# An adaptive LoRA and feed-forward kernel in split fp32: a sum ahead of a split in the first pair, a low-rank product ahead of the tails' mixing in the second, VectorE's filling increments left out

## The reference

```python
# layer 1: y = x W^T + 2 * sum over the two best experts of gate * (x A_e^T) B_e^T
logits = x @ Wr.T + 5.0 * one_hot(language)        # 8 experts
topw, topi = top_k(logits, 2)
gates = softmax(topw) put at topi
y = x @ W.T + 2.0 * einsum(x @ A, gates, B)        # rank 16
# layer 2: 4 experts, all of them weighted by a softmax
g = softmax(y @ Wr2.T)
z = y @ W2.T + b + 2.0 * einsum(y @ A2, g, Bm)     # rank 8
return x + z
```

## Time and profile before

| what | value |
|---|---|
| median of three runs | 327.86 us |
| the profiled execution, its own time | 328.54 us |
| its span, first to last instruction | 326.8 us |
| TensorE matmuls busy | 319.5 us, 98% |
| TensorE weight loads busy | 314.0 us, 96% |
| VectorE busy | 245.4 us, 75% |
| ScalarE busy | 128.2 us, 39% |
| mean granted clock of TensorE | 0.997 of full speed |
| share of TensorE in the chain that ended last | 94% |

### The profile page before, as it was taken

The page is one execution under the profiler, slowest core; times in us unless marked ns, Lnnn a source line. Parts: engine busy times, 40 slices in busy tenths (PEclk is TensorE's granted clock), DMA queues, the critical chain, the costliest instruction groups (busy, mean ns, idle before and its releaser), DMA issues.

```text
span 326.8 us, 5993 instructions
## 1 busy us (share of the span) xinstructions
PE 319.5 (98%) x2255; PEld 314.0 (96%) x2255; DVE 245.4 (75%) x541; ACT 128.2 (39%) x253; POOL 1.4 (0%) x11
## 2 busy tenths in 40 slices
PE   7999999999999999999999999999999999999994
PEld 6999999999998998899999999999999999999993
DVE  3989999998899778978866856857666685684442
ACT  4872846495148226226413503512431350341120
POOL 1000000000000000000000000000000000000000
PEclk9999999999999999999999999999999999999998
DMA  7999000000000311700420340150061024003004
GB/s 230 421 406 299 6 2 0 2 0 2 0 2 0 130 39 37 252 0 0 143 118 0 76 181 0 52 205 0 0 196 61 0 75 182 0 0 128 0 0 129
DMA packets 10559, 27.56 MB, mean 84 GB/s; under 512 B 3150, under 2 KB 4430, under 8 KB 10544
## 3 DMA queue, kind: packets, MB, share of 16 engines
q1 hardware_dynamic: 10256, 27.18, 24.0%
q10 hardware_dynamic: 288, 0.19, 0.2%
HBM read 18.97 MB, written 8.39 MB: 84 GB/s over the span
## 4 chain that ended last, share of the span: by engine, by line
PE 94%; DVE 2%; DMA 1%; ACT 1%; issue 0%; SPq 0%; DVEq 0%
PE sums L1273 94%; DMA in<-part 1%; PE sums L1512 1%; DVE rows L1048 0%; DVE st_low L771 0%; DVE vt_plain L1214 0%; ACT vt L527 0%; ACT y_exp L719 0%; DVE a_low L771 0%; DVE v L1203 0%; ACT a_high L527 0%; SPq L430 0%; SPq L428 0%; DVE sec L1194 0%; DVE y_half L1200 0%
## 5 line engine op out<-in xcount | busy, mean ns | idle before, releaser
L1273 PE MATMUL sums<-b_high,a_high 128*128 128x256 f32 (+1 forms) x224 | 45.5, 287 | 1.0 <-DVE a_low L771 1.0
L1273 PE MATMUL sums<-b_low,a_high 128*128 128x256 f32 (+1 forms) x224 | 45.4, 286 | 0.0
L1273 PE MATMUL sums<-b_high,a_low 128*128 128x256 f32 (+1 forms) x224 | 45.3, 286 | 0.0
L1273 PEld LDWEIGHTS sums<-b_high,a_high 128*128 128x128 f32 x224 | 34.7, 189 | 1.5 <-DVE a_low L771 1.2
L1273 PEld LDWEIGHTS sums<-b_low,a_high 128*128 128x128 f32 x224 | 34.8, 189 | 0.0
L1273 PEld LDWEIGHTS sums<-b_high,a_low 128*128 128x128 f32 x224 | 34.7, 188 | 0.1
L1048 DVE TENSOR_TENSOR rows<-sums,rows 128x354 f32<-128x354 f32 x48 | 24.4, 521 | 9.7 <-PE sums L1273 9.3
L1273 PE MATMUL sums<-t_high,s_high 128*128 128x354 f32 x96 | 31.6, 330 | 0.0
L1273 PE MATMUL sums<-t_low,s_high 128*128 128x354 f32 x96 | 31.1, 324 | 0.0
L1273 PE MATMUL sums<-t_high,s_low 128*128 128x354 f32 x96 | 31.1, 324 | 0.0
L1048 DVE TENSOR_TENSOR narrow<-sums,narrow 128x244 f32<-128x244 f32 x30 | 12.4, 412 | 24.3 <-PE sums L1273 24.3
(11 more groups left out here) (150 smaller groups left out, 823.0 us busy)
## 6 DMA issues: line engine op xcount, KB each, us to landing
stage<-tokens SPq DMA_DIRECT2D x14, 512.0 KB, 4.0
out<-rows SPq DMA_DIRECT2D x14, 512.0 KB, 4.7
in<-part SPq DMA_DIRECT2D x7, 585.0 KB, 8.4
in<-part SPq DMA_DIRECT2D x4, 777.0 KB, 15.7
in<-part SPq DMA_DIRECT2D x4, 265.0 KB, 18.6
rows<-tokens SPq DMA_DIRECT2D x2, 512.0 KB, 15.8
c_plain<-gate_proj SPq DMA_DIRECT2D x1, 544.0 KB, 17.8
c_plain<-gate_proj SPq DMA_DIRECT2D x4, 136.0 KB, 3.0
```

The costliest lines, as they stand in the source:

```text
L1273: return nc.tensor.matmul(out_, lhs, rhs, start=start, stop=stop, skip_group_check=True)
```

## The change

`STEPS` becomes 10, which is the number of links, and the increments that filled up to 14 go. In the first pair `add_r22` now comes before `split_x(j + 1, 0)` on VectorE; in the second it stays where it was, ahead of `split_tn(T4)`. On TensorE the second pair now has lora for bank B ahead of the tails' mixing, as the first had.

```diff
@@ -1047,7 +1047,7 @@
             def add_sums(dst, n, onto):
                 return nc.vector.tensor_tensor(dst, n, onto, ALU.add)
 
-            STEPS = 14
+            STEPS = 10
             BLOCK = 32
 
             def pair(j, first=False, second=False, last=False):
@@ -1218,13 +1218,13 @@
                     add_r22()
                 dve.wait_ge(v_rounded, j + 1)
                 low_part(vt[ER2:2 * ER2, :, :], vt_plain[:, :, :], vt[0:ER2, :, :]).then_inc(vt_ready, 1)
+                if not steady:
+                    add_r22()
                 if second:
-                    add_r22()
                     split_tn(T4)
                 if not last:
                     split_x(j + 1, 0)
                 if first:
-                    add_r22()
                     next_s(S1)
                     next_s(S2)
                 if second:
@@ -1257,9 +1257,7 @@
                     split_s(j + 1, S3)
                 dve.wait_ge(c_done, j + 1)
                 add_sums(rows[:, 0, wide_at(1)], bank(BANK_C), rows[:, 0, wide_at(1)]).then_inc(c_out, 1)
-                assert step[0] <= STEPS, step
-                for _ in range(STEPS - step[0]):
-                    dve.sem_inc(vec, 1)
+                assert step[0] == STEPS, step
 
             pair(0, first=True)
             pair(1, second=True)
@@ -1547,7 +1545,7 @@
                     pe.wait_ge(t_split, T4 + 1)
                 pe.wait_ge(u3_read, j + 1)
                 of_x(BANK_B, 1, 1, t_high[T4], t_low[T4], False).then_inc(p4_done, 1)
-                if first:
+                if not steady:
                     lora(BANK_B, 1, 0)
                     mixed_tails(j)
                 else:
```

## The result

The changed kernel takes 326.49 us (median of six runs, 326.01 to 326.84) against 327.86 us (six runs, 327.74 to 328.24); the ratio is 0.9953, 95% interval 0.9943 to 0.9964. It is faster by 1.37 us by the medians, and by 1.2 to 1.9 us by the interval of the ratio. I had forecast 326.92 us and a range down to 326.65.

What follows compares the result with a forecast made beforehand. TensorE, busy for 98% of the span, was taken to bound the kernel, so only its standstills could be won. The terms 0.69 + 0.25 + 0 = 0.94 us, off the median 327.86, gave 326.92 us, range 326.65 to 327.45.

Steps and rivals of the forecast that it cites:

- Part 1: First pair: add_r22 ahead of the split of x on VectorE removes TensorE's wait; 0.69 us, bounds 0.45 and 0.7.
- The restart: First pair, TensorE's step behind the wait at product 3: 0.24 instead of 0.16 us, so 0.08 us more gained.
- The bare 0.61 us: Gain in the first pair's stretch, product 4 to product 3, if the weight load were done in the gap.
- Part 2: Second pair: lora ahead of mixed_tails on TensorE makes the wait for vt vanish; 0.25 us, bounds 0 and 0.3.
- What is late next: Logits before the gate: wanted at 139.47, VectorE free at 139.44, so the first pair's gain passes with 0.03 us spare.
- The first rival: Second pair's VectorE list falls behind the earlier TensorE; gain 0.45 to 0.65, time 327.2 to 327.4 us; chance 0.18.
- The second: Second pair: the tails' mixing finds another wait or vt comes later; gain 0.69, time 327.17 us; chance 0.05.
- the fourth: TensorE meets u3_read of the second pair without slack; freed VectorE gives 0.1 to 0.3 more, 326.7 us; chance 0.05.
- Part 3: Four filling increments fewer per pair on VectorE, 32 in a run: costed at nothing, upper bound 0.38 us per pass.
- The third rival: Shorter VectorE program exposes a late fetch now hidden at 127 to 140 us; 2.9 us, time 329.8; chance 0.04.

## Why the prediction was right on both moves and wrong on the increments

**Part 1** was right: 0.69 us forecast, 0.66 measured between the transposes, 0.67 in the run with this part alone. The restart was part of it, as the step of 0.17 us in place of 0.24 shows. The bare 0.61 us that I gave for a weight load done in the gap is less than both measurements.

**Part 2** was right: 0.25 forecast, 0.24 measured, both in the whole change and alone. The copy of the tails started at 153.69 in the changed profile and held nobody up.

**What is late next** was right, to the hundredth of which it spoke: the logits came at 139.49 on the old scale, forecast 139.47, and VectorE had just ended. With 0.03 us to spare, that nothing was held back was partly luck. The first rival, a gate chain that holds the gain back, didn't come: TensorE has no wait behind 7 us. The second and the fourth did not come either. The first narrow matmul of pair 2 stands at 156.55, with the start's 0.55 added 157.10, as forecast. (The chances that I added up for "faster" come to 0.71, not 0.73.)

**Part 3** failed. The term was "I cost them at nothing", with a bound of 0.38 us per pass "and VectorE isn't on the path there". On TensorE's path that is so: 205.22 us with 14 and with 10 steps, 205.24 with 26. On VectorE the bound turned out to be about the whole cost: at the seam of two passes leaving four increments out saved 0.41 us (0.90 to 0.49). The 0.43 us from 132.20 to 132.63 that spoke for no cost are the end of the first pair, not the second's, and hold outside the loop only. What I took for the whole path was TensorE's; the 4.7 us behind it, the last output and the wait for it, I took as a constant that lies around the sum. There 16 instructions fewer in VectorE's text are worth 0.56 us (10 steps alone, ratio 0.9983; and 0.9970 against 0.9953 with both moves).

I had the mechanism in hand and put it at the wrong place with the wrong sign. The third rival says that a shorter text moves a fetch of VectorE's program and that this could make things *slower*, with one in the middle of the run coming into the open. I read the packet from 127 to 140 us, which is one of `q8`, a queue that VectorE's text doesn't move. The packet that mattered is one of `q14`, in the last 5 us, where its removal could only help. A view from 240 to 327 us, taken before the prediction, had listed it, without its place; I didn't ask further. With the half microsecond that the runs give this term, the sum would have been 0.94 + 0.5 and the time 326.4 us.

Of the Trainium skill's passage that I named there (Advanced Engine Details and Errata, ISA Cache: lines of 16 KB or 256 instructions, two of them held) the runs show only that text is fetched in blocks: 48 instructions more in VectorE's text clear the end again and 12 more than the changed kernel's bring the packet back, in line with a border whose place was not located. The packets of this queue carry 8 KB (14 GB/s over 0.6 us), half of the line that the page gives.

Added up: 0.90 us from the moves and 0.5 to 0.6 from the fetch are 1.4 to 1.5 us; the medians say 1.37, the ratio of the first runs 1.5 and that of the repeated ones 1.5. The 0.55 us at the start of the profiled execution are not the change's.

**What stays open.** That the packet carries VectorE's text is inferred from what moves it, not read from its content. That it shares a DMA engine with the late packets is inferred from their times; the engines are not shown one by one. What sets the packet's moment is known in part: it starts at 1.7 us where nothing stands behind the last sum and at 2.1 us with four increments there, but at 2.5 us with four in the changed kernel. There is one profile of each kernel (two of the changed one), so how far packet and end vary between executions of one kernel is not known; whether the larger remainder with 26 steps (0.9 us) differs from 0.6 can't be told from these intervals.

## What to carry to other kernels

Where TensorE is full, the gain of a reordering is the excess of its stretch over the same stretch in an undisturbed pass of the loop, restart included. This gave both moves to 0.03 us. The path doesn't end with the last matmul: ask for the DMA queues of the last few microseconds too, and look for an instruction packet among the packets of the last output. If there is one, a change in the length of an engine's program, even instructions that do nothing, can move it away, and any edit that changes a length should be compared against one that keeps it.

## What the runs showed of the hardware that I had not expected

- A kernel became faster by 0.85 us (ratio 0.9974) when 96 increments that do nothing were added to its run. In its profile the instruction packet had gone from the last output to about 308 us.
- The delay depends on the packet's moment within half a microsecond. In the profiles where it started 1.7 to 2.1 us behind the start of the last sum, the last small packet of the output came at 2.5 to 3.0 us in place of 2.0, and the kernels lacked 0.6 to 0.9 us by their ratios. Where it started at 2.5 us, they didn't (326.48 us).
- An instruction packet of 8 KB took between 0.4 and 0.9 us of one DMA engine's time.
- A stand-alone increment on VectorE took some 0.1 us at the seam of two passes (0.49, 0.90 and 1.86 us with none, four and sixteen), and nothing at the end of the first pair (0.44, 0.43 and 0.43 us). In TensorE's path it left no trace: 205.22, 205.22 and 205.24 us with 10, 14 and 26 steps.
